# An eight-core two-layer transformer: FP4 absolute values moved to VectorE, the normalisation front split in two halves, and a constant row broadcast earlier

## The chip, the cores and the metric

The kernel runs on the 8 cores of one Trainium2 chip. Each core computes one of the 8 sequences of the batch with the same program; the cores exchange nothing. The metric is device time in microseconds (us) of the slowest core. Engines are named TensorE (PE in the profile), VectorE (DVE), ScalarE (ACT), GpSimd (POOL) and SyncE (SP, which here only issues DMAs).

## The reference

Two pre-norm layers over x of [8, 2048, 1024]. `_layernorm` here has no gain; layer 1's attention adds a second layer norm with `ln_gamma` and `ln_beta` after its own residual. The feed-forward part of layer 1 is what most of the change is about.

```python
x = x + attn0(layernorm(x))          # 16 heads, decay mask on the scores
x = x + fp6_linear(layernorm(x))     # 1024 -> 1024, blocks of 32
x = x + attn1(layernorm(x))          # its result: LN(u + attn_out) * gamma + beta
x = x + ffn1(layernorm(x))

def fp4_quant_dequant(x):            # blocks of 16 along the last dim
    scale = max(max(|xb|) / 6.0, 1e-12)
    xn = xb / scale
    idx = searchsorted([0.25, 0.75, 1.25, 1.75, 2.5, 3.5, 5.0], |xn|)
    return GRID[idx] * sign(xn) * scale
def ffn1(x):                         # H = 1024, I = 2816
    gate = fp4(x) @ fp4(w_gate).T
    y    = fp4(x) @ fp4(w_up).T
    return fp4(silu(gate) * y) @ fp4(w_down).T
```

## The kernel before

A core has 2048 rows, cut in 16 tiles of 128 rows (`NT` = 16, t = 0 to 15), one row to a partition. The program is four stages with a barrier between them: attention 0, the FP6 feed-forward layer, attention 1, the FP4 feed-forward layer (`emit_ffn1`). Intermediate results go through DRAM (`xs1` to `xs3`). The FP4 weights are quantized beforehand, in pieces woven into attention 1, by the same `emit_quant_fp4` on VectorE with 512 or 352 columns (the tiles named `pw_`).

A helper class, `Prog`, records every operation with the names of what it reads and writes, and sets semaphore waits from them. What it does not do is reorder: each engine's queue holds its operations in the order in which the Python code emits them, and an engine that waits holds back all that stands behind. The reader needs that order at every step.

`emit_ffn1` works on a tile in three parts.

- `front(t)`: load x of the tile (SyncE's queue), layer norm (`ln_stats_and_u`: a sum on VectorE at L160, a square with accumulation on ScalarE at L163, a power on GpSimd at L178, the normalised u32 by ScalarE at L182), then FP4 quantization of u32 in two halves of 512 columns into `xqb` (bf16), then eight 128x128 transposes on TensorE (L1227) through two PSUM tiles `ptr0` and `ptr1`, each copied out by ScalarE (L1230) into `xqf`.
- `back_mid(t)`: six slices k of the 2816 columns, five of 512 and one of 256. For each: eight gate matmuls (L1245), Silu on ScalarE (L1252) into `gs`, eight up matmuls (L1258), a copy on ScalarE (L1265), their product on GpSimd (L1269) back into `gs`, and FP4 quantization of `gs` on VectorE into `hq`. There are two each of the PSUM tiles `pg` and `pu`, of `gs`, and of `upe`.
- `back_down(t)`: 22 transposes of `hq` on TensorE (L1282) through the same `ptr0` and `ptr1`, each copied by ScalarE (L1285) into `hqT`; two groups of 22 matmuls of 512 columns (L1296) into `pd0` and `pd1`; an add to x on VectorE after each group (L1301); the store.

The order of the stage is written out by hand: `front(0)`, `front(1)`, `back_mid(0)`, and then for each t: `front(t+2)`, `back_mid(t+1)`, `back_down(t)`. Buffers of x and `xqf` rotate over three tiles, so x of tile t+2 goes where tile t-1 was stored from.

`emit_quant_fp4` is a chain of VectorE operations on scratch tiles that all quantizations of the stage share: block maximum (L217), scale (L220), reciprocal (L223), product y (L229), absolute value u, then four comparisons with thresholds (L240 and three times L244), three more with sums (L247 to L256), and the assembling of the result (L259 to L270). The absolute value is an activation on ScalarE (L232) when `abs_eng` is "scalar", as in all of `emit_ffn1`, and a `scalar_tensor_tensor` on VectorE (L236) by default, as in the weight preparation.

In attention 1, the row with gamma and beta is broadcast over the 128 partitions by four small fp32 matmuls with a row of ones into the one PSUM tile `pq` (L928), each copied out by ScalarE (L932) into `gb_b`. This stands after the attention proper, just before the output projection (L962), whose weights `wo` are loaded there too. `gb_b` is read by VectorE at L989 and L991. The stage begins with sixteen layer norms, whose x loads are at L700.

Of the kernel before, what the change touches and what calls it, by code (L numbers as in the profile page):

```python
# [9 lines left out]
F32 = mybir.dt.float32  # L10
BF16 = mybir.dt.bfloat16
F16 = mybir.dt.float16
AF = mybir.ActivationFunctionType
# [5 lines left out]
D = 1024  # L19
NT = T // 128  # L20
NC = D // 128
# [130 lines left out]
def ln_stats_and_u(p, xt_ap, xkey, sq_scr, sqkey, stats, stkey, col, u_out, ukey,  # L152
                   extra_u=None, rstd_via="act"):
    ncol = stats.shape[1] // 4
    s1 = stats[:, col:col + 1]
    rstd = stats[:, ncol + col:ncol + col + 1]
    negmr = stats[:, 2 * ncol + col:2 * ncol + col + 1]
    ssq = stats[:, 3 * ncol + col:3 * ncol + col + 1]
    kst = stkey + str(col) + "_"
    p.op("vector", lambda e: e.reduce_sum(s1, xt_ap, AX.X), ins=[xkey], outs=[kst + "s1"])  # L160
    p.op("vector", lambda e: e.tensor_scalar_mul(s1, s1, -1.0 / D),
         ins=[kst + "s1"], outs=[kst + "s1"])
    p.op("scalar", lambda e: e.activation(out=sq_scr, in_=xt_ap, func=AF.Square,  # L163
                                          bias=s1, accum_out=ssq),
         ins=[xkey, kst + "s1"], outs=[sqkey, kst + "ssq"])
    if rstd_via == "act":
        p.op("scalar", lambda e: e.activation(out=rstd, in_=ssq, func=AF.Ln,
                                              scale=np.float32(1.0 / D),
                                              bias=np.float32(LNEPS)),
             ins=[kst + "ssq"], outs=[kst + "rstd"])  # L170
        p.op("scalar", lambda e: e.activation(out=rstd, in_=rstd, func=AF.Exp,
                                              scale=np.float32(-0.5)),
             ins=[kst + "rstd"], outs=[kst + "rstd"])
    else:
        p.op("vector", lambda e: e.tensor_scalar(rstd, ssq, 1.0 / D, LNEPS,
                                                 ALU.mult, ALU.add),
             ins=[kst + "ssq"], outs=[kst + "rstd"])
        p.op("gpsimd", lambda e: e.tensor_tensor(rstd, rstd, p.mh[:], ALU.pow),  # L178
             ins=[kst + "rstd", "mh"], outs=[kst + "rstd"])
    p.op("vector", lambda e: e.tensor_mul(negmr, s1, rstd),  # L180
         ins=[kst + "s1", kst + "rstd"], outs=[kst + "negmr"])
    p.op("scalar", lambda e: e.activation(out=u_out, in_=xt_ap, func=AF.Identity,  # L182
                                          scale=rstd, bias=negmr),
         ins=[xkey, kst + "rstd", kst + "negmr"], outs=[ukey])
    if extra_u is not None:
        ap2, key2 = extra_u
        p.op("scalar", lambda e: e.activation(out=ap2, in_=xt_ap, func=AF.Identity,
                                              scale=rstd, bias=negmr),
             ins=[xkey, kst + "rstd", kst + "negmr"], outs=[key2])
# [395 lines left out]
def emit_attn(p, dram, layer, prep=None, prep2=None):  # L585
# [7 lines left out]
    x_d, y_d, eye_d = dram["x"], dram["y"], dram["eye"]  # L593
# [6 lines left out]
    else:  # L600
        gb_d = dram["gb"]
# [7 lines left out]
    ones32 = p.sb("ones32", [1, 128], F32)  # L609
# [49 lines left out]
    if layer == 0:  # L659
# [28 lines left out]
                                              func=AF.Identity, bias=np.float32(0.0)),  # L688
             ins=["pq"], outs=["ball"])

    outer_actx = p.actx
    with ExitStack() as sc1:
        p.actx = sc1
# [55 lines left out]
    for hp in range(NHP):  # L749
# [166 lines left out]
        in_=woT_d.ap().rearrange("(c p) f -> p c f", p=128)),  # L916
        outs=["wo"])
    if layer == 1:
        gb_b = p.sb("gb_b", [128, 2 * D], F32)
        u32 = [p.sb("u32_s", [128, D], F32)] * 2  # L920
        ysb = p.sb("ysb", [128, D], F32)
        p.dma("sync", "c_gb", lambda e: e.dma_start(out=gb_b[0:1, :],
                                                    in_=gb_d.ap()),
              outs=["gbrow"])
        for half in range(2):
            for fs in range(0, D, 512):
                o = half * D + fs
                p.op("tensor", lambda e, o=o: e.matmul(  # L928
                    pq[:, 0:512], ones32[0:1, :], gb_b[0:1, o:o + 512],
                    start=True, stop=True),  # L930
                    ins=["gbrow", "ones32"], outs=["pq"])
                p.op("scalar", lambda e, o=o: e.activation(  # L932
                    out=gb_b[:, o:o + 512], in_=pq[:, 0:512],
                    func=AF.Identity, bias=np.float32(0.0)),
                    ins=["pq"], outs=["gb_b"])
    if "dbg_attn" in dram:
        p.dma("sync", "dbg1", lambda e: e.dma_start(out=dram["dbg_attn"].ap(),
                                                    in_=attn[:]), ins=attn_all,
# [226 lines left out]
def emit_ffn1(p, dram, prep_done=False):  # L1165
# [45 lines left out]

    ISL = [(k * 512, min((k + 1) * 512, I_DIM)) for k in range(6)]

    def front(t):
        bi, ri = t % 2, t % 3
        p.dma("sync", f"x{ri}", lambda e, t=t, ri=ri: e.dma_start(
            out=xt[ri][:], in_=x_d.ap()[t * 128:(t + 1) * 128, :]),
            outs=[f"xt{ri}"])
        ln_stats_and_u(p, xt[ri][:], f"xt{ri}", u32[bi][:], "u32s",
                       stats, "st", bi, u32[bi][:], "u32s", rstd_via="pool")  # L1220
        for h in range(2):
            emit_quant_fp4(p, u32[bi][:, h * 512:(h + 1) * 512], "u32s",
                           xqb[bi][:, h * 512:(h + 1) * 512], f"xqb{bi}",
                           scr, "qs", 32, abs_eng="scalar")
        for ec in range(NC):
            pk = "ptr" + str(ec % 2)
            p.op("tensor", lambda e, ec=ec, bi=bi: e.transpose(  # L1227
                ptr[ec % 2][:], xqb[bi][:, ec * 128:(ec + 1) * 128], eye[:]),
                ins=[f"xqb{bi}", "eye"], outs=[pk])
            p.op("scalar", lambda e, ec=ec, ri=ri: e.activation(  # L1230
                out=xqf[ri][:, ec * 128:(ec + 1) * 128],
                in_=ptr[ec % 2][:], func=AF.Identity, bias=np.float32(0.0)),
                ins=[pk], outs=[f"xqf{ri}_{ec}"])

    def back_mid(t):
        bi, ri = t % 2, t % 3
        xqf_all = [f"xqf{ri}_{ec}" for ec in range(NC)]
        for k, (i0, i1) in enumerate(ISL):
            isl = slice(i0, i1)
            pgk, kpg = pg[k % 2], f"pg{k % 2}"  # L1240
            puk, kpu = pu[k % 2], f"pu{k % 2}"

            def mmg(e, isl=isl, i0=i0, i1=i1, ri=ri, pgk=pgk):
                for ec in range(NC):
                    inst = e.matmul(pgk[:, 0:i1 - i0],  # L1245
                                    xqf[ri][:, ec * 128:(ec + 1) * 128],
                                    wgT[:, ec * I_DIM:(ec + 1) * I_DIM][:, isl],
                                    start=(ec == 0), stop=(ec == NC - 1))
                return inst
            p.op("tensor", mmg, ins=xqf_all + wgT_all, outs=[kpg])  # L1250
            p.op("scalar", lambda e, i0=i0, i1=i1, k=k,
                 pgk=pgk: e.activation(  # L1252
                out=gs[k % 2][:, 0:i1 - i0], in_=pgk[:, 0:i1 - i0], func=AF.Silu),
                ins=[kpg], outs=[f"gsb{k % 2}"])

            def mmu(e, isl=isl, i0=i0, i1=i1, ri=ri, puk=puk):
                for ec in range(NC):
                    inst = e.matmul(puk[:, 0:i1 - i0],  # L1258
                                    xqf[ri][:, ec * 128:(ec + 1) * 128],
                                    wuT[:, ec * I_DIM:(ec + 1) * I_DIM][:, isl],  # L1260
                                    start=(ec == 0), stop=(ec == NC - 1))
                return inst
            p.op("tensor", mmu, ins=xqf_all + wuT_all, outs=[kpu])
            usl = slice((k % 2) * 512, (k % 2) * 512 + (i1 - i0))
            p.op("scalar", lambda e, usl=usl, i0=i0, i1=i1, puk=puk: e.activation(  # L1265
                out=upe[:, usl], in_=puk[:, 0:i1 - i0], func=AF.Identity,
                bias=np.float32(0.0)),
                ins=[kpu], outs=[f"upe{k % 2}"])
            p.op("gpsimd", lambda e, usl=usl, k=k, i0=i0, i1=i1: e.tensor_tensor(  # L1269
                gs[k % 2][:, 0:i1 - i0], upe[:, usl], gs[k % 2][:, 0:i1 - i0],  # L1270
                ALU.mult),
                ins=[f"upe{k % 2}", f"gsb{k % 2}"], outs=[f"gsb{k % 2}"])
            emit_quant_fp4(p, gs[k % 2][:, 0:i1 - i0], [f"gsb{k % 2}"],
                           hq[bi][:, isl], f"hq{bi}s_{k}", scr, "qs",
                           (i1 - i0) // 16, abs_eng="scalar")

    def back_down(t):
        bi, ri = t % 2, t % 3
# [31 lines left out]
    back_mid(0)  # L1310
    for t in range(NT):
        if t + 2 < NT:
            front(t + 2)
        if t + 1 < NT:
            back_mid(t + 1)
        back_down(t)


# [133 lines left out]
```

How the kernel before makes its waits and increments, by code:

```python
                def body(e):  # L124
                    for waits, fn, ch in recs_:
                        for typ, a, c in waits:
                            if typ == "e":
                                e.wait_ge(self.sem[a], c)
                            else:
                                e.wait_ge(self.dsem[a], 16 * c)
                        if fn is None:
                            continue
                        inst = fn(e)
                        if ch is None:
                            inst.then_inc(self.sem[eng_], 1)
                        else:
                            inst.then_inc(self.dsem[ch], 16)
```

## Time and profile before

| | |
|---|---|
| median of 3 runs | 7549.77 us (7544.5 to 7551.43) |
| the profiled execution's own time | 7555.49 us |
| its span on the slowest core (core 4), first to last instruction | 7553.9 us |
| spans of the eight cores | 7530.0 to 7553.9 us |
| VectorE, ScalarE, TensorE matmul, GpSimd busy | 62%, 29%, 38%, 2% |
| FP4 feed-forward stage, from its first weight transposes | about 5340 to 7554 us |

The profile is one execution, on the slowest core; times in it are us from the start of that core's span. About 1.6 us of the execution's time lie outside of the span. A busy share is an average over all stages. Waits are inferred from semaphores: the engine named is the one that released last.

### The profile page before, as it was taken

Reading aid. Unit: us, or ns where it says so; the run is one execution under the profiler, and the core shown is the slowest. Engines: PE = TensorE matmul, PEld = TensorE weight load, DVE = VectorE, ACT = ScalarE, POOL = GpSimd, SP = SyncE. Lnnn points to the kernel's source line nnn. Section 1 sums busy time; section 2 is a strip of 40 time slices with the busy share of each in tenths; the row PEclk is TensorE's granted clock in tenths of the full one; section 3 lists DMA queues with packets and bytes.
Section 4 is the critical chain, followed back from the end, with each engine's and each line's share of the span. In section 5 each row is a group of like instructions: output and inputs, shape, how many; then the busy total and the mean of one; then the engine's idle time right before and its main releaser. Section 6 shows DMA issues by size and latency. Waiting matters only on the chain.

```text
span 7553.9 us, 51889 instructions; the slowest of 8 cores (7530.0 to 7553.9 us)
## 1 busy us (share of the span) xinstructions
PE 2850.0 (38%) x9802; PEld 943.0 (12%) x9802; DVE 4647.5 (62%) x8046; ACT 2178.5 (29%) x3098; POOL 187.3 (2%) x193
## 2 busy tenths in 40 slices
PE   2645544445540111284343344223023333333334
PEld 1111111111110000021111111000011111111111
DVE  3555555555437777368888888843275665656555
ACT  2244544444500110244343345312111111111111
POOL 0000000000000000000000000000000000000000
PEclk9655555555575555587676677656565656656566
DMA  3000000000031110211111111111500000000000
GB/s 74 6 6 6 1 6 6 6 4 3 1 104 29 36 36 34 67 32 37 36 35 37 35 29 28 29 49 46 114 0 11 6 6 12 6 11 6 11 6 9
DMA packets 194787, 192.26 MB, mean 25 GB/s; under 512 B 120627, under 2 KB 156467, under 8 KB 194355
## 3 DMA queue, kind: packets, MB, share of 16 engines
q1 hardware_dynamic: 77332, 144.37, 5.8%
q0 software_dynamic: 39904, 25.18, 2.2%
q10 hardware_dynamic: 77248, 19.40, 1.5%
q8 instruction: 101, 1.65, 0.1%
q14 instruction: 202, 1.65, 0.1%
HBM read 133.35 MB, written 52.95 MB: 25 GB/s over the span
## 4 chain that ended last, share of the span: by engine, by line
DVE 52%; PE 15%; ACT 12%; issue 12%; DMA 6%; ACTq 2%; DVEq 2%; POOL 1%; SPq 0%; POOLq 0%
DVE f_qs_a L244 4%; DVE f_pw_a L244 4%; ACT a_ebf L829 4%; DVE a_msk L826 3%; PE a_po L843 3%; PE f_pd L1296 3%; PE a_psW L810 2%; PE a_pq L730 2%; PE a_po L848 2%; DVEq L128 2%; ACTq L564 2%; DMA f_xt<-xs 1%; DVE f_pw_y L229 1%; DVE f_pw_b L256 1%; DVE f_pw_u L236 1%
## 5 line engine op out<-in xcount | busy, mean ns | idle before, releaser
L826 DVE TENSOR_TENSOR a_msk<-a_psW,a_emask 128x1024 f32<-128x1024 f32 x512 | 623.7, 1224 | 436.8 <-PE a_psW L814 375.9
L843 PE MATMUL a_po<-a_ebf,a_v_all 128*65 128x512 bf16 x1024 | 507.4, 496 | 934.3 <-ACT a_ebf L829 777.3
L829 ACT ACTIVATE a_ebf<-a_msk 128x1024 bf16<-128x1024 f32 x512 | 541.0, 1057 | 586.5 <-DVE a_msk L826 442.3
L833 ACT ACTIVATE a_ebf<-a_psW 128x1024 bf16<-128x1024 f32 x512 | 515.0, 1023 | 110.6 <-PE a_psW L814 90.1
L848 PE MATMUL a_po<-a_ebf,a_v_all 128*65 128x512 bf16 x1024 | 516.3, 504 | 0.0
L810 PE MATMUL a_psW<-a_qp,a_kp 64*128 64x512 bf16 x1024 | 507.0, 507 | 15.6 <-ACT a_kp L776 8.4
L814 PE MATMUL a_psW<-a_qp,a_kp 64*128 64x512 bf16 x1024 | 507.5, 508 | 0.0
L232 ACT ACTIVATE f_qs_u<-f_qs_y 128x512 f32<-128x512 f32 (+1 forms) x128 | 77.1, 602 | 1134.3 <-DVE f_qs_y L229 1134.3
L244 DVE SCALAR_TENSOR_TENSOR f_qs_a<-f_qs_u,f_qs_a 128x512 f32<-128x512 f32 (+1 forms) x384 | 313.9, 817 | 40.3 <-DVE f_qs_a L244 0.5
L894 PE MATMUL a_pq<-a_dbf,a_ones 1*64 1x512 bf16 x64 | 38.4, 600 | 764.3 <-ACT a_dbf L885 764.3
L1245 PE MATMUL f_pg<-f_wgT,f_xqf 128*128 128x512 bf16 (+1 forms) x768 | 233.8, 465 | 235.2 <-ACT f_gs L1252 235.2
L244 DVE SCALAR_TENSOR_TENSOR f_pw_a<-f_pw_u,f_pw_a 128x512 f32<-128x512 f32 (+1 forms) x456 | 283.6, 622 | 49.9 <-DVE f_pw_a L244 1.8
L1227 PE MATMUL f_ptr<-f_eye,f_xqb 128*128 128x128 bf16 x128 | 30.5, 264 | 739.6 <-DVE f_xqb L270 719.2
L1087 PE MATMUL f_ptr<-f_eye,f_xqb 128*128 128x128 bf16 x128 | 32.5, 264 | 713.1 <-DVE f_xqb L346 693.6
L1282 PE MATMUL f_ptr<-f_eye,f_hq 128*128 128x128 bf16 x352 | 88.6, 266 | 535.8 <-ACT f_hqT L1285 527.3
L843 PEld LDWEIGHTS a_po<-a_ebf,a_v_all 128*65 128x65 bf16 x1024 | 122.3, 119 | 1349.1 <-issue 1349.1
L962 PE MATMUL a_psW<-a_wo,a_attn 128*128 128x512 bf16 x512 | 164.5, 479 | 279.3 <-DVE a_ysb L984 218.9
L769 PE MATMUL a_pq<-a_u_fm,a_wqkv 128*128 128x512 bf16 x1024 | 256.5, 418 | 0.0
L866 ACT ACTIVATE a_asb<-a_po 64x512 f32<-64x512 f32 x64 | 37.8, 591 | 630.5 <-DVE a_attn L878 629.6
L1258 PE MATMUL f_pu<-f_wuT,f_xqf 128*128 128x512 bf16 (+1 forms) x768 | 203.5, 418 | 0.0
L1296 PE MATMUL f_pd<-f_wdT,f_hqT 128*128 128x512 bf16 x704 | 194.5, 447 | 8.5 <-ACT f_hqT L1285 8.5
L1090 ACT ACTIVATE f_xqf<-f_ptr 128x128 bf16<-128x128 bf16 x128 | 33.7, 277 | 552.7 <-PE f_ptr L1087 551.5
(196 smaller groups left out, 6072.1 us busy)
## 6 DMA issues: line engine op xcount, KB each, us to landing
xs<-a_xtw SPq DMA_DIRECT2D x32, 512.0 KB, 2.6
f_xt<-xs SPq DMA_DIRECT2D x32, 512.0 KB, 3.8
f_pw_wch<-f_wg SPq DMA_DIRECT2D x44, 256.0 KB, 2.8
f_pw_wch<-f_wu SPq DMA_DIRECT2D x44, 256.0 KB, 2.8
f_pw_wch<-f_wd SPq DMA_DIRECT2D x64, 176.0 KB, 2.4
a_xt<-x SPq DMA_DIRECT2D x16, 512.0 KB, 3.8
a_xtw<-x SPq DMA_DIRECT2D x16, 512.0 KB, 3.5
f_xtw<-xs POOLq DMA_DIRECT2D x16, 512.0 KB, 3.6
```

What stands on the lines that cost most here:

```text
L244: p.op("vector", lambda e, th=th: e.scalar_tensor_tensor(out=a[:, 0:W], in0=u[:, 0:W], scalar=th, in1=a[:, 0:W], op0=ALU.is_gt, op1=ALU.ad ...
L769: inst = e.matmul(psel[:], wqkv[wb][:, j * D + c * 128: j * D + c * 128 + 128], u_fm[:, c * T:(c + 1) * T][:, sl], start=(c == 0), stop=(c ...
L810: p.op("tensor", lambda e, kc=kc, psx=psx, qsl=qsl: e.matmul(psx[:, 0:512], kp[0:64, kc * 128:(kc + 1) * 128], qp[0:64, qsl], start=True, ...
L814: p.op("tensor", lambda e, kc=kc, psx=psx, qsl=qsl: e.matmul(psx[:, 512:1024], kp[64:128, kc * 128:(kc + 1) * 128], qp[64:128, qsl], start ...
L826: p.op("vector", lambda e, m3=m3, p3=p3, e3=e3: e.tensor_tensor(m3, p3, e3, ALU.mult), ins=[kA, kB, "emask0", "emask1"], outs=[f"mskp{par}"])
L829: p.op("scalar", lambda e, esl=esl: e.activation(out=ebf[:, esl], in_=msk[:, esl], func=AF.Exp), ins=[f"mskp{par}"], outs=[ek])
L833: p.op("scalar", lambda e, psx=psx, esl=esl: e.activation(out=ebf[:, esl], in_=psx[:], func=AF.Exp, scale=np.float32(0.125)), ins=[kA, kB] ...
L843: p.op("tensor", lambda e, kc=kc, eo=eo, vb=vb: e.matmul(po0[0:65, :], v_all[:, vb: vb + 65], ebf[:, eo: eo + 512], start=(kc == 0), stop= ...
L848: p.op("tensor", lambda e, kc=kc, eo=eo, vb=vb: e.matmul(po1[0:65, :], v_all[:, vb + 65: vb + 130], ebf[:, eo + 512: eo + 1024], start=(kc ...
L1245: inst = e.matmul(pgk[:, 0:i1 - i0], xqf[ri][:, ec * 128:(ec + 1) * 128], wgT[:, ec * I_DIM:(ec + 1) * I_DIM][:, isl], start=(ec == 0), st ...
L1258: inst = e.matmul(puk[:, 0:i1 - i0], xqf[ri][:, ec * 128:(ec + 1) * 128], wuT[:, ec * I_DIM:(ec + 1) * I_DIM][:, isl], start=(ec == 0), st ...
L1296: inst = e.matmul(psx[:], hqT[:, ic * 128:(ic + 1) * 128], wdT[:, ic * D:(ic + 1) * D][:, fsl], start=(ic == 0), stop=(ic == NI - 1))
```

## The change

It does four things.

- In `emit_ffn1` all quantizations take the absolute value on VectorE (L236) in place of ScalarE (L232): `abs_eng="scalar"` goes away in both calls.
- `front(t)` becomes `front_half(t, 0)` and `front_half(t, 1)`. Half 0 has the load, the layer norm, the quantization of columns 0 to 511 and the first four transposes with their copies; half 1 has the quantization of columns 512 to 1023 and the other four.
- In the loop, half 0 of tile t+2 stays ahead of `back_mid(t+1)`, and half 1 comes after it, ahead of `back_down(t)`. The two fronts at the start of the stage have both halves in a row.
- In attention 1 the load, the four matmuls and the four copies of gamma and beta go to the beginning of the stage, ahead of the sixteen layer norms; `gb_b` is held from there on.

```diff
--- before.py
+++ after.py
@@ -688,6 +688,23 @@
                                               func=AF.Identity, bias=np.float32(0.0)),
              ins=["pq"], outs=["ball"])
 
+    if layer == 1:
+        gb_b = p.sb("gb_b", [128, 2 * D], F32)
+        p.dma("sync", "c_gb", lambda e: e.dma_start(out=gb_b[0:1, :],
+                                                    in_=gb_d.ap()),
+              outs=["gbrow"])
+        for half in range(2):
+            for fs in range(0, D, 512):
+                o = half * D + fs
+                p.op("tensor", lambda e, o=o: e.matmul(
+                    pq[:, 0:512], ones32[0:1, :], gb_b[0:1, o:o + 512],
+                    start=True, stop=True),
+                    ins=["gbrow", "ones32"], outs=["pq"])
+                p.op("scalar", lambda e, o=o: e.activation(
+                    out=gb_b[:, o:o + 512], in_=pq[:, 0:512],
+                    func=AF.Identity, bias=np.float32(0.0)),
+                    ins=["pq"], outs=["gb_b"])
+
     outer_actx = p.actx
     with ExitStack() as sc1:
         p.actx = sc1
@@ -916,23 +933,8 @@
         in_=woT_d.ap().rearrange("(c p) f -> p c f", p=128)),
         outs=["wo"])
     if layer == 1:
-        gb_b = p.sb("gb_b", [128, 2 * D], F32)
         u32 = [p.sb("u32_s", [128, D], F32)] * 2
         ysb = p.sb("ysb", [128, D], F32)
-        p.dma("sync", "c_gb", lambda e: e.dma_start(out=gb_b[0:1, :],
-                                                    in_=gb_d.ap()),
-              outs=["gbrow"])
-        for half in range(2):
-            for fs in range(0, D, 512):
-                o = half * D + fs
-                p.op("tensor", lambda e, o=o: e.matmul(
-                    pq[:, 0:512], ones32[0:1, :], gb_b[0:1, o:o + 512],
-                    start=True, stop=True),
-                    ins=["gbrow", "ones32"], outs=["pq"])
-                p.op("scalar", lambda e, o=o: e.activation(
-                    out=gb_b[:, o:o + 512], in_=pq[:, 0:512],
-                    func=AF.Identity, bias=np.float32(0.0)),
-                    ins=["pq"], outs=["gb_b"])
     if "dbg_attn" in dram:
         p.dma("sync", "dbg1", lambda e: e.dma_start(out=dram["dbg_attn"].ap(),
                                                     in_=attn[:]), ins=attn_all,
@@ -1211,18 +1213,18 @@
 
     ISL = [(k * 512, min((k + 1) * 512, I_DIM)) for k in range(6)]
 
-    def front(t):
+    def front_half(t, h):
         bi, ri = t % 2, t % 3
-        p.dma("sync", f"x{ri}", lambda e, t=t, ri=ri: e.dma_start(
-            out=xt[ri][:], in_=x_d.ap()[t * 128:(t + 1) * 128, :]),
-            outs=[f"xt{ri}"])
-        ln_stats_and_u(p, xt[ri][:], f"xt{ri}", u32[bi][:], "u32s",
-                       stats, "st", bi, u32[bi][:], "u32s", rstd_via="pool")
-        for h in range(2):
-            emit_quant_fp4(p, u32[bi][:, h * 512:(h + 1) * 512], "u32s",
-                           xqb[bi][:, h * 512:(h + 1) * 512], f"xqb{bi}",
-                           scr, "qs", 32, abs_eng="scalar")
-        for ec in range(NC):
+        if h == 0:
+            p.dma("sync", f"x{ri}", lambda e, t=t, ri=ri: e.dma_start(
+                out=xt[ri][:], in_=x_d.ap()[t * 128:(t + 1) * 128, :]),
+                outs=[f"xt{ri}"])
+            ln_stats_and_u(p, xt[ri][:], f"xt{ri}", u32[bi][:], "u32s",
+                           stats, "st", bi, u32[bi][:], "u32s", rstd_via="pool")
+        emit_quant_fp4(p, u32[bi][:, h * 512:(h + 1) * 512], "u32s",
+                       xqb[bi][:, h * 512:(h + 1) * 512], f"xqb{bi}",
+                       scr, "qs", 32)
+        for ec in range(h * 4, h * 4 + 4):
             pk = "ptr" + str(ec % 2)
             p.op("tensor", lambda e, ec=ec, bi=bi: e.transpose(
                 ptr[ec % 2][:], xqb[bi][:, ec * 128:(ec + 1) * 128], eye[:]),
@@ -1231,6 +1233,10 @@
                 out=xqf[ri][:, ec * 128:(ec + 1) * 128],
                 in_=ptr[ec % 2][:], func=AF.Identity, bias=np.float32(0.0)),
                 ins=[pk], outs=[f"xqf{ri}_{ec}"])
+
+    def front(t):
+        front_half(t, 0)
+        front_half(t, 1)
 
     def back_mid(t):
         bi, ri = t % 2, t % 3
@@ -1272,7 +1278,7 @@
                 ins=[f"upe{k % 2}", f"gsb{k % 2}"], outs=[f"gsb{k % 2}"])
             emit_quant_fp4(p, gs[k % 2][:, 0:i1 - i0], [f"gsb{k % 2}"],
                            hq[bi][:, isl], f"hq{bi}s_{k}", scr, "qs",
-                           (i1 - i0) // 16, abs_eng="scalar")
+                           (i1 - i0) // 16)
 
     def back_down(t):
         bi, ri = t % 2, t % 3
@@ -1310,9 +1316,11 @@
     back_mid(0)
     for t in range(NT):
         if t + 2 < NT:
-            front(t + 2)
+            front_half(t + 2, 0)
         if t + 1 < NT:
             back_mid(t + 1)
+        if t + 2 < NT:
+            front_half(t + 2, 1)
         back_down(t)
```

## Rows read from the trace of the kernel before

**Rows 1.** The page, parts 1 and 4: busy time by engine, the chain that ended last.

```profile
PE 2850.0 (38%) x9802; PEld 943.0 (12%) x9802; DVE 4647.5 (62%) x8046; ACT 2178.5 (29%) x3098; POOL 187.3 (2%) x193
...
DVE 52%; PE 15%; ACT 12%; issue 12%; DMA 6%; ACTq 2%; DVEq 2%; POOL 1%; SPq 0%; POOLq 0%
```

**Rows 2.** Waits in the last stage: who waited for whom, total us, times, longest.

```profile
DVE f_xt L1301 <- PE f_pd L1296: 249.3, 31, 16.0
...
DVE f_qs_bm L217 <- POOL f_gs L1269: 177.0, 16, 11.7
```

**Rows 3.** Timeline of one tile, VectorE: start, us, engine, line, operation, [idle before <-releaser].

```profile
5609.29 0.69 DVE L270 TENSOR_TENSOR f_xqb<-f_qs_a,f_qs_b 128x512 bf16<-128x512 f32 x1
...
5620.64 0.69 DVE L217 TENSOR_REDUCE f_qs_bm<-f_gs 128x32 f32<-128x512 f32 x1 [10.66 <-POOL f_gs L1269]
...
5689.73 0.42 DVE L270 TENSOR_TENSOR f_hq<-f_qs_a,f_qs_b 128x256 bf16<-128x256 f32 x1
...
5701.18 0.69 DVE L1301 TENSOR_TENSOR f_xt<-f_pd,f_xt 128x512 f32<-128x512 f32 x1 [11.02 <-PE f_pd L1296]
...
5705.99 0.69 DVE L1301 TENSOR_TENSOR f_xt<-f_pd,f_xt 128x512 f32<-128x512 f32 x1 [4.12 <-PE f_pd L1296]
...
5752.99 0.69 DVE L217 TENSOR_REDUCE f_qs_bm<-f_gs 128x32 f32<-128x512 f32 x1 [11.42 <-POOL f_gs L1269]
```

**Rows 4.** Timeline of the same tile, TensorE.

```profile
5610.12 0.37 PE L1227 MATMUL f_ptr<-f_eye,f_xqb 128*128 128x128 bf16 x2 [66.91 <-DVE f_xqb L270]
...
5613.08 3.62 PE L1245 MATMUL f_pg<-f_wgT,f_xqf 128*128 128x512 bf16 x8
...
5684.80 0.50 PE L1282 MATMUL f_ptr<-f_eye,f_hq 128*128 128x128 bf16 x2 [31.82 <-ACT f_hqT L1285]
...
5693.92 11.90 PE L1296 MATMUL f_pd<-f_wdT,f_hqT 128*128 128x512 bf16 x44 [0.52 <-ACT f_hqT L1285]
```

**Rows 5.** Timeline: one quantization of the last stage, and one of the weight preparation.

```profile
4908.68 0.53 DVE L236 SCALAR_TENSOR_TENSOR f_pw_u<-f_pw_y 128x352 f32<-128x352 f32 x1
4909.31 0.34 DVE L240 TENSOR_SCALAR f_pw_a<-f_pw_u 128x352 f32<-128x352 f32 x1
...
5634.61 0.69 DVE L229 TENSOR_TENSOR f_qs_y<-f_gs,f_qs_bm 128x512 f32<-128x512 f32 x1
...
5636.13 0.43 DVE L240 TENSOR_SCALAR f_qs_a<-f_qs_u 128x512 f32<-128x512 f32 x1 [0.83 <-ACT f_qs_u L232]
...
5636.66 3.15 DVE L244 SCALAR_TENSOR_TENSOR f_qs_a<-f_qs_u,f_qs_a 128x512 f32<-128x512 f32 x3
...
5637.14 1.33 POOL L1269 TENSOR_TENSOR f_gs<-f_upe,f_gs 128x512 f32<-128x512 f32 x1 [11.10 <-ACT f_upe L1265]
```

**Rows 6.** Timeline of the last two tiles.

```profile
7482.43 0.59 ACT L1265 ACTIVATE f_upe<-f_pu 128x512 f32<-128x512 f32 x1
...
7510.87 0.42 DVE L270 TENSOR_TENSOR f_hq<-f_qs_a,f_qs_b 128x256 bf16<-128x256 f32 x1
...
7538.17 11.38 PE L1296 MATMUL f_pd<-f_wdT,f_hqT 128*128 128x512 bf16 x44 [0.62 <-ACT f_hqT L1285]
...
7549.73 0.69 DVE L1301 TENSOR_TENSOR f_xt<-f_pd,f_xt 128x512 f32<-128x512 f32 x1 [4.13 <-PE f_pd L1296]
```

**Rows 7.** Timeline of layer 1's attention: its start, and gamma and beta's place.

```profile
3060.35 0.91 SPq L700 DMA_DIRECT2D a_xt<-xs  x2
...
3065.52 1.15 ACT L163 ACTIVATE a_msk<-a_xt,a_stats 128x1024 f32<-128x1024 f32 x1 [24.63 <-DVE a_stats L161]
...
4975.09 0.26 SPq L922 DMA_DIRECT2D a_gb_b<-a_gb  x1
...
4978.29 2.04 PE L928 MATMUL a_pq<-a_gb_b,a_ones 1*128 1x512 f32 x2 [117.07 <-DMA a_gb_b<-a_gb]
...
4989.39 0.60 ACT L932 ACTIVATE a_gb_b<-a_pq 128x512 f32<-128x512 f32 x1 [2.38 <-PE a_pq L928]
...
4991.69 3.57 PE L962 MATMUL a_psW<-a_wo,a_attn 128*128 128x512 bf16 x8 [2.40 <-DMA a_wo<-a_woT]
```

## The prediction

> **What bounds the kernel now.** I read the page first, for the shares. VectorE is busy 62% of the span and holds 52% of the chain that ended last [rows 1]; no other engine comes near. Most of the diff is in the last stage (the FP4 feed-forward layer), so I then read the waits of VectorE in that stage [rows 2]. Two recur once per tile: the residual adds (L1301) wait for the down projection, 249.3 us over 31 waits, and the first quantization of a tile (L217) waits for the gate and up results through GpSimd, 177.0 us over 16. Then I followed one tile in the timeline [rows 3]. It begins at 5620.64 and the next begins at 5752.99, so a tile takes 132.35 us: six quantizations of `back_mid` (to 5690.15), 11.02 us of wait, one add, 4.12 us of wait, one add (to 5706.68), a layer norm and two quantizations of `front`, and 11.42 us of wait. VectorE is either working or waiting for a chain that its own last result started. So the stage is serial, and the question for each edit is what it does to these waits.
>
> Why they exist is in the queues of TensorE and ScalarE [rows 4]. TensorE stood idle for 66.91 us until `front(t+2)`'s last quantization wrote `xqb`, and then ran its transposes and after them `back_mid(t+1)`'s gate matmuls at 5613.08. Those need only activations of tile t+1, ready one tile before; they waited because they stand behind the transposes. TensorE takes its queue strictly in the order of the program. At 5684.80 the transposes of `hq` (tile t) resume after 31.82 us, released by ScalarE: the copies out of PSUM (L1285) stand behind the last absolute value (L232) of tile t+1, which waits for VectorE. The down projection starts at 5693.92, and its first half frees the add at 5701.18.
>
> **Absolute value on VectorE (128 quantizations of the last stage).** Now L240 starts 1.52 us after L229 (5634.61 to 5636.13), of which 0.83 us is idle for ScalarE's result [rows 5]. After, L236 stands between them. No row has it with 512 columns. The weight preparation has it with 352: 0.53 us, and L240 follows 0.63 us after it, a gap of 0.10. L229 itself takes 0.69 for 512, on two operands as L236 has. So 0.69 + 0.10, twice, is 1.58 us: +0.06 for each of seven full quantizations of a tile, and about +0.02 for the one of 256 columns, in all +0.44 us per tile. Bounds: 0 (the idle time is just filled), and 0.2 for each (a gap twice as long on both sides), 1.5 per tile.
>
> Perfetto Trace Analysis of the Trainium skill, section Optimizing Scalar/DVE Operations, speaks against this edit: when VectorE is saturated, offloading some work to ScalarE may make sense. The trace doesn't bear it out here, since VectorE waits 0.83 us for what was offloaded.
>
> GpSimd's multiply (L1269) is moved too. It runs beside L244 [rows 5]: the three L244 take 3.15 us where 3 x 0.69 + 2 x 0.10 = 2.27 would do, so it costs VectorE 0.88 us, four times per tile (0.3 for the fifth, short one). Without the absolute value in ScalarE's queue, the Silu and the copy that feed it run about 0.54 us earlier, and the multiply starts at some 5636.6 instead of 5637.14, just ahead of the first L244 instead of late in it. VectorE then stands blocked from closer to the multiply's beginning: I estimate +0.18 each, +0.7 per tile. Bounds: -0.88 (no overlap) and +0.45 (blocked for the whole 1.33), so -3.5 to +1.8 per tile.
>
> The SBUF — State Buffer page of the Trainium skill, under Who interferes with whom, says that VectorE and GpSimd share a port pair as an exclusive lock. By that rule a multiply costs VectorE at most its own 1.33 us; the sum would be the upper bound just given.
>
> The larger effect is on order: ScalarE's copies of `hq` no longer stand behind the last absolute value. By itself this would let them run during `back_mid(t+1)`.
>
> **Split front (14 tiles have it).** After quantizing half 0, only four transposes are queued before `back_mid(t+1)`'s gate matmuls. Eight took 5613.08 - 5610.12 = 2.96 us from first to gate; in steady pace a pair starts every 0.89 us, so four fewer are 1.8 us: the wait of 11.42 shrinks to 9.6. Bound: 0.9, if the clock (0.43 us per matmul, the 1.2 GHz level, in the gate group that took 3.62 us) rises no earlier than it does now. I take -1.8.
>
> But half 1's quantization now comes after all six of `back_mid(t+1)`, and its four transposes stand in TensorE's queue ahead of `back_down(t)`'s 22. So `hq(t)` is held until VectorE has ended half 1; VectorE's next instruction is the add that needs the down projection. Nothing covers it. From the end of half 1: 0.15 us to the first transpose (as before 5610.12); 26 transposes in 13 pairs. Twenty took 5693.92 - 5684.80 = 9.12 us to the down projection; six more at 0.445 each give 11.8. Then 5701.18 - 5693.92 = 7.26 to the add. That is 19.2 us of wait in place of 11.02: +8.2 us. The second wait, 4.12, stays. What was gained on ScalarE is unused, because the copies wait for transposes that TensorE has not run. The next tile's x load stays behind the store, as now.
>
> Per tile: +8.2 - 1.8 + 0.44 + 0.7 = +7.5 us, and 14 tiles give +105. The start (two fronts, one `back_mid`) gives -1.8 + 0.6 + 0.7 = -0.5.
>
> **The end.** Tiles 14 and 15 have no front above them, so there ScalarE's freedom counts [rows 6]. The last quantization of tile 15 ends at 7511.29. ScalarE reached the copy of slice 4 at 7482.43; with the absolute values gone slice 5's is done about then. 22 transposes (10 us) and 12.8 us of down projection of tile 14 are over by about 7506, and 20 of tile 15's transposes by 7515. Its down projection starts near 7515.3 instead of 7538.17: -22.9, and +1.2 for the quantizations before it: -21.7.
>
> **Gamma and beta.** Four rounds of matmul and copy took 4978.29 to 4989.99, 11.7 us, beginning 3.2 us after the row's DMA was issued at 4975.09 [rows 7]. At their old place they are free: the output projection starts at 4991.69 when its weights land. At the new one ScalarE's first square (3065.52) stands behind them. The row is issued where now the first x load is, at 3060.35, so they end near 3075.1: +9.6. VectorE's next step needs that square, so nothing hides it. I add 0.6 for a first output projection without the warm-up that those matmuls gave: +10.2. Bounds: 8 to 11.5.
>
> **Sum.** 105 - 0.5 - 21.7 + 10.2 = +93 us. The profiled execution took 7555.49, 5.7 over the median; +93 on it is 7648.5, and on the median 7549.8 it is 7643.
>
> **Rivals.**
> - *The down projection hides under the second half* (ends faster). If the `hq(t)` transposes ran while VectorE quantizes tile t+1, the 11.02 and 4.12 would vanish: -15.1 - 1.8 + 0.44 + 0.7 = -15.8 per tile, -221 for 14; with the other terms -233, that is 7317. This decides at one point: whether they get ahead of the four second-half transposes. For it: their data are ready a tile early, and ScalarE is free. Against it: the 66.91 us of idle TensorE with ready work queued behind [rows 4]. 6 in 100.
> - *The low clock lasts through the down projection.* All 44 matmuls at 0.43 would take 18.9 us instead of 12.8, from 5693.92 to 5706.68: +6.1, for 14 tiles +86, 7729. The transposes before it are sparse now too, and the rise came inside it, so I give 5 in 100.
> - *VectorE pays the absolute value in full*, as the rule on offloading has it: 112 x 0.69 + 16 x 0.42 = 84 us instead of 7, giving 7720. The 0.83 of idle time speaks against it. 3 in 100.
> - *It about cancels.* The multiplies stop colliding (64 x 0.88 + 16 x 0.3 = -61 us, and -11 that I had added), which leaves +21, 7571. If TensorE's clock rises early in the down projection as well (2.7 us of low clock saved is 1.3 per tile, -18), it is +3, 7553. 6 in 100, two thirds of it within 0.2%.
> - The forecast has 80 in 100.
>
> **How the numbers follow.** Against the values taken, the multiplies' bounds are -59 and +15 us over 14 tiles, those of the absolute value -6 and +15, that of the split's saving +13, and a clock that rises 2.7 us earlier or later in the down projection is 18 either way. All at once is unlikely; half of each is -42 and +31, and I widen the upper side to +42, since late clocks and late multiplies would come together. That gives 7600 to 7685, which should hold 8 in 10 over all cases: the forecast nearly whole, and little of the rivals. 0.2% is 15 us, about what a measurement of this kernel can tell from no change. Faster 0.06, same 0.04, slower 0.90.
>
> **What would show it.** The adds' first wait should read about 19 us per tile instead of 11, released by a down projection that starts some 12 us after half 1's last write. L217's wait should be near 9.6. TensorE should stand idle through `back_mid(t+1)` until L1227's second half, and L1282 should never run before it except in tile 14. L240 should wait for nothing. The layer's first square should start near 3075. The forecast is wrong if L1282 runs beside `back_mid`, if the three L244 change their 3.15 us by more than half, or if the down projection takes over 15 us.

## The result, and the profile after

The changed kernel takes 7624.55 us (median of 8 runs, 7612.9 to 7652.61) against 7550.78 us before (8 runs, 7544.5 to 7565.5): a ratio of 1.01, 95% interval 1.0085 to 1.0114. It is slower by 74 us; the forecast was slower by 93, 7643 in a range of 7600 to 7685.

The page's busy times and chain hardly tell the two kernels apart [rows 1]. VectorE is busy 94 us more, ScalarE 67 less:

```profile
PE 2789.1 (37%) x9802; PEld 929.5 (12%) x9802; DVE 4741.6 (62%) x8174; ACT 2111.3 (28%) x2970; POOL 180.8 (2%) x193
...
DVE 53%; PE 16%; issue 11%; ACT 11%; DMA 5%; ACTq 2%; DVEq 2%; POOL 1%; SPq 0%; POOLq 0%
```

The waits of VectorE in the last stage do (total us, times, longest). They answer to [rows 2]: the adds' wait for the down projection grew from 249.3 to 341.0, the first quantization's fell from 177.0 to 146.1.

```profile
DVE f_xt L1307 <- PE f_pd L1302: 341.0, 30, 19.5
...
DVE f_qs_bm L217 <- POOL f_gs L1275: 146.1, 16, 9.8
```

One tile on VectorE, as in [rows 3]. The first row is now half 1's last write, the next two are the adds, and the last begins the next tile:

```profile
5674.40 0.69 DVE L270 TENSOR_TENSOR f_xqb<-f_qs_a,f_qs_b 128x512 bf16<-128x512 f32 x1
...
5694.38 0.69 DVE L1307 TENSOR_TENSOR f_xt<-f_pd,f_xt 128x512 f32<-128x512 f32 x1 [19.29 <-PE f_pd L1302]
...
5699.20 0.69 DVE L1307 TENSOR_TENSOR f_xt<-f_pd,f_xt 128x512 f32<-128x512 f32 x1 [4.12 <-PE f_pd L1302]
...
5732.73 0.69 DVE L217 TENSOR_REDUCE f_qs_bm<-f_gs 128x32 f32<-128x512 f32 x1 [9.39 <-POOL f_gs L1275]
```

And TensorE, as in [rows 4]:

```profile
5675.24 0.37 PE L1229 MATMUL f_ptr<-f_eye,f_xqb 128*128 128x128 bf16 x2 [62.80 <-DVE f_xqb L270]
...
5677.01 0.52 PE L1288 MATMUL f_ptr<-f_eye,f_hq 128*128 128x128 bf16 x2 [0.40 <-ACT f_xqf L1232]
...
5687.19 11.83 PE L1302 MATMUL f_pd<-f_wdT,f_hqT 128*128 128x512 bf16 x44 [0.52 <-ACT f_hqT L1291]
```

TensorE waits 62.80 us for half 1, runs four transposes, begins the 22 of `hq` at 5677.01 and the down projection at 5687.19. The add waits 19.29 us, behind nothing but these. Where [rows 4] had ScalarE as the releaser of the `hq` transposes after 31.82 us, TensorE's own queue now holds them.

From the traces' times I worked out stretches of the stages, as means over the eight cores, in us. Each runs from one DMA issue or first instruction to the next.

```
stretch                                                 before    after
attention 1: load of bq to load of the v weights          141.6    150.6
attention 1: to the load of the output weights           1775.5   1766.1
attention 1: to the last stage's first weight transpose   364.4    363.4
last stage: to the first square of a layer norm            99.0     99.3
last stage: to the first quantization of back_mid          69.4     65.6
last stage: from there to the end                        2042.9   2118.3
```

Two things stand out. The last row has the loss, 75 us. And attention 1 lost 9 us at its beginning and found them again in its middle, where the change touches nothing.

### The profile page after: what moved, and what is told of

The parts are those of the page before. It is cut to its first block, busy times and chain, and to the rows that moved or that the text cites. A ratio compares the mean times of both kernels' runs of the same rounds, so it can differ in the third digit from the quotient of the medians.

```text
span 7614.2 us, 51936 instructions; the slowest of 8 cores (7602.4 to 7614.2 us)
## 1 busy us (share of the span) xinstructions
PE 2789.1 (37%) x9802; PEld 929.5 (12%) x9802; DVE 4741.6 (62%) x8174; ACT 2111.3 (28%) x2970; POOL 180.8 (2%) x193
## 4 chain that ended last, share of the span: by engine, by line
DVE 53%; PE 16%; issue 11%; ACT 11%; DMA 5%; ACTq 2%; DVEq 2%; POOL 1%; SPq 0%; POOLq 0%
DVE f_qs_a L244 4%; ACT a_ebf L846 4%; DVE f_pw_a L244 4%; PE a_po L860 3%; DVE a_msk L843 3%; PE a_psW L827 2%; PE f_pd L1302 2%; PE a_po L865 2%; DVEq L128 2%; PE a_pq L747 2%; ACTq L564 1%; DVE f_qs_u L236 1%; DMA f_xt<-xs 1%; DVE f_pw_y L229 1%; DVE f_pw_u L236 1%
## 5 line engine op out<-in xcount | busy, mean ns | idle before, releaser
L850 ACT ACTIVATE a_ebf<-a_psW 128x1024 bf16<-128x1024 f32 x512 | 511.2, 1023 | 114.3 <-PE a_psW L831 94.8
L244 DVE SCALAR_TENSOR_TENSOR f_qs_a<-f_qs_u,f_qs_a 128x512 f32<-128x512 f32 (+1 forms) x384 | 299.2, 779 | 41.4 <-DVE f_qs_a L244 1.8
L244 DVE SCALAR_TENSOR_TENSOR f_pw_a<-f_pw_u,f_pw_a 128x512 f32<-128x512 f32 (+1 forms) x456 | 283.6, 622 | 47.5
L1307 DVE TENSOR_TENSOR f_xt<-f_pd,f_xt 128x512 f32<-128x512 f32 x32 | 22.1, 692 | 341.1 <-PE f_pd L1302 341.0
L1251 PE MATMUL f_pg<-f_wgT,f_xqf 128*128 128x512 bf16 (+1 forms) x768 | 204.8, 420 | 80.4 <-ACT f_gs L1258 80.4
L1258 ACT ACTIVATE f_gs<-f_pg 128x512 f32<-128x512 f32 x96 | 53.9, 562 | 632.0 <-DVE f_qs_y L229 537.0
```

The source lines that it names most:

```text
L244: p.op("vector", lambda e, th=th: e.scalar_tensor_tensor(out=a[:, 0:W], in0=u[:, 0:W], scalar=th, in1=a[:, 0:W], op0=ALU.is_gt, op1=ALU.ad ...
L850: p.op("scalar", lambda e, psx=psx, esl=esl: e.activation(out=ebf[:, esl], in_=psx[:], func=AF.Exp, scale=np.float32(0.125)), ins=[kA, kB] ...
L1251: inst = e.matmul(pgk[:, 0:i1 - i0], xqf[ri][:, ec * 128:(ec + 1) * 128], wgT[:, ec * I_DIM:(ec + 1) * I_DIM][:, isl], start=(ec == 0), st ...
```

## Experiments

Ratios are to the kernel before, run on the same chip.

**1. Gamma and beta early, nothing else.** The diff's first hunk and the removal of its lines at the old place.

> The kernel before with gamma and beta's broadcast moved to the beginning of attention 1, nothing else. By the sum of the prediction the first square of the stage starts some 9 us later and nothing hides it: about +9 us, near 7560, and the span from the stage's first load to the output projection's weights is 9 us longer. The rival comes from the changed kernel's profile, where attention 1 as a whole was not longer (2280.1 us against 2281.5, means over cores) though its beginning was by 9: by that the 9 us are given back later in the stage, 7550, and the eight head pairs should then each be about 1.2 us shorter here too. If the head pairs take what they took before, the difference in the changed kernel was one of executions.

Measured: 7547.86 us, ratio 1.0001 (0.9993 to 1.001). My sum's +9 did not come, and its rival held. The beginning of attention 1 is 8.9 us longer (150.5), its middle 9.2 us shorter (1766.3): the changed kernel's finding again, and spread over all eight head pairs, 0.3 to 1.6 us each. So it belongs to the edit, and is no accident of an execution. What it is, runs 5 and 6 ask.

**2. Absolute values on VectorE alone.**

```diff
-                           scr, "qs", 32, abs_eng="scalar")
+                           scr, "qs", 32)
...
-                           (i1 - i0) // 16, abs_eng="scalar")
+                           (i1 - i0) // 16)
```

> The kernel before with all absolute values of the last stage on VectorE, fronts whole, gamma and beta where they were. My theory: ScalarE's copies of hq now run beside back_mid, so the adds' waits (15.1 us per tile) vanish, against +0.9 us per tile in back_mid: about -14.4 us for 14 tiles and -22 at the end, near 7327. The rival that VectorE pays the absolute value in full (77 us) and the copies gain nothing gives 7627.

Measured: 7313.12 us, ratio 0.969 (0.9677 to 0.9703). Its waits on VectorE in the last stage:

```profile
DVE f_qs_bm L217 <- POOL f_gs L1269: 165.2, 15, 12.0
...
DVE f_xt L1301 <- PE f_pd L1296: 13.0, 2, 8.9
```

The adds wait twice, at the end of the program, and never else. A tile takes 118.1 us instead of 133.0. Against the kernel before on the same chip (7548.45 us) this edit was worth 235 us, and in the change it earned only the end of the program.

**3. The split alone**, absolute values on ScalarE.

> The kernel before with the front split as in the change, absolute values on ScalarE, gamma and beta where they were. My theory (half 1's four transposes hold back the 22 of back_down in TensorE's queue): from the end of back_mid to the second add +8.0 us beyond the moved quantization, first wait of a tile -2.0, so +6.0 for 14 tiles, about +82, near 7632, with nothing gained at the end (39 us from the last quantization to the last add, as before). If the absolute value were what costs, this would be at or below 7530.

Measured: 7627.6 us, ratio 1.0106 (1.009 to 1.0121).

```profile
DVE f_xt L1305 <- PE f_pd L1300: 361.6, 31, 20.3
DVE f_qs_bm L217 <- POOL f_gs L1273: 145.5, 16, 9.9
```

361.6 and 145.5 us, the pattern of the changed kernel. From the last quantization to the last add it takes 39.0 us, as before the change.

**4. The changed kernel, half 1's four transposes behind `back_down`.**

```diff
         if t + 2 < NT:
             front_half(t + 2, 1)      # its quantization only
         back_down(t)
+        if t + 2 < NT:
+            front_tr(t + 2, 1)        # its four transposes and copies
```

> The changed kernel with one thing moved: half 1 is quantized where the change has it, but its four transposes stand behind back_down's work in TensorE's and ScalarE's queues. My theory says that these four are the whole cause: the adds' wait of 19.3 + 4.1 us goes to nothing and a tile takes about 116.5 us instead of 140.0, near 7296 in all. If instead TensorE's clock or VectorE's extra work were behind the slower tile, it would stay near 7620.

Measured: 7291.57 us, ratio 0.9659 (0.9646 to 0.9673).

```profile
DVE f_qs_bm L217 <- POOL f_gs L1281: 142.8, 16, 9.9
...
DVE f_xt L1313 <- PE f_pd L1308: 12.4, 2, 8.3
```

A tile takes 116.1 us. VectorE does the same work in the same order as in the changed kernel; only four transposes per tile, with their copies, have another place in TensorE's and ScalarE's queues, and the time falls by 333 us.

**5 and 6. One more VectorE instruction.** In the traces, the 9 us found again are small idle times of VectorE inside the weight preparation. Where two operations of a quantization usually stand 0.10 us apart, at some places it is 0.46, as in this row of the kernel before (VectorE's timeline at the second such place, [idle before]):

```profile
3403.51 0.35 DVE L223 RECIPROCAL f_pw_bm<-f_pw_bm 128x32 f32<-128x32 f32 x1 [0.46 <-DVE f_pw_bm L220]
```

The place is not bound to an operation. Numbering all entries of VectorE's instruction list from 0 (waits too), every such stall of every kernel sits at an entry number that is 59 modulo 128, and this entry is an operation with its wait just ahead of it. The weight preparation has 41 entries with such a number. In the kernel before 35 of them are operations, of which 29 stall; in the changed one 8 are, and 4 stall. The others have no wait just ahead, but for three L217. The edit for both runs:

```diff
+    if layer == 1:
+        fill = p.sb("fill", [1, 1], F32)
+        p.op("vector", lambda e: e.memset(fill[:], 0.0), outs=["fill"])
```

> The kernel before with one more instruction for VectorE, a memset of one element at the beginning of attention 1, which needs about 0.1 us. In the traces so far VectorE stands idle for 0.46 us in the weight preparation 29 times in each kernel with gamma and beta in their old place, 4 times in each with them at the new one, on every core alike, and each time at an entry of its instruction list whose number is 59 modulo 128; the two kinds of kernels differ there by one entry. Theory: where the entry that follows such a place is the operation itself and not its wait, 0.46 us is exposed, and one more entry takes 25 of the 29 stalls away: about -9 us, near 7540, with 4 stalls. The rival (the place of gb_b in memory, or the clock) expects no change, 7549, with 29.

> The changed kernel with the same one-element memset. Theory: the 4 stalls of its weight preparation become some 29 again or another number between, at most +9 us, near 7633. The rival expects 7624 and 4 stalls.

Measured, kernel before with the memset: 7539.14 us, ratio 0.9987 (0.9978 to 0.9996), 4 stalls on every core, and the middle of attention 1 takes 1766.5 us instead of 1775.5. Changed kernel with it: 7630.43 us, ratio 1.011 (1.0096 to 1.0124), 29 stalls, and the middle takes 1773.7 instead of 1766.1. Its time alone could not be told from the changed kernel's; the stretch and the stalls can. Of the waits of VectorE on its own last result, the kernel before with the memset keeps four rows between 3200 and 4975 us (its waits of 0.5 us are the 4 stalls; the three of L223, of 0.3 each, stand just behind an entry numbered 59 that is a wait, where part of the stall still shows), where the changed one with it has eleven, which make up the 29, and of which the first four are:

```profile
DVE f_pw_b L250 <- DVE f_pw_b L247: 0.9, 2, 0.5
DVE f_pw_bm L223 <- DVE f_pw_bm L220: 0.8, 3, 0.3
DVE f_pw_b L263 <- DVE f_pw_b L259: 0.5, 1, 0.5
DVE f_pw_a L268 <- DVE f_pw_u L265: 0.5, 1, 0.5
```

```profile
DVE f_pw_a L244 <- DVE f_pw_a L244: 2.3, 5, 0.5
DVE f_pw_wqb L270 <- DVE f_pw_a L268: 1.8, 4, 0.5
DVE f_pw_u L236 <- DVE f_pw_y L229: 1.4, 3, 0.5
DVE f_pw_bm L223 <- DVE f_pw_bm L220: 1.4, 3, 0.5
...
```

So the place of VectorE's entries is the cause of the 9 us: the same memset takes the stalls from one kernel and gives them to the other. What moved the list by one entry in the change is the broadcast's DMA: its channel is waited for at the barrier after the layer norms, one wait more ahead of the preparation and one fewer after it (16301 entries in the kernel before and in run 1).

**7. Transposes late, fronts whole**, on the kernel before with the absolute values on VectorE:

```diff
         if t + 2 < NT:
-            front(t + 2)
+            front_dve(t + 2)          # load, layer norm, both quantizations
         if t + 1 < NT:
             back_mid(t + 1)
+        if t + 2 < NT:
+            front_tr(t + 2)           # eight transposes and copies
         back_down(t)
```

> The kernel before with absolute values on VectorE, and fronts whole but for their eight transposes, which stand between back_mid(t+1) and back_down(t). My theory of in-order queues: the gate matmuls of tile t+1 no longer stand behind transposes that wait for VectorE, so the wait of about 11.4 us ahead of the first quantization vanishes besides the adds' waits: a tile takes 106.9 us where it took 118.2 with the absolute values alone, near 7155 in all. The rival is that the 30 transposes with their copies and the down projection no longer fit beside back_mid(t+1); then the adds wait again for some us per tile, 7155 to 7250.

Measured: 7171.07 us, ratio 0.95 (0.9487 to 0.9513). The adds and the first quantization wait twice each, outside of the steady tiles. A tile takes 107.8 us where I expected 106.9. Of this 0.9 us, 0.5 is that the wait that vanished was 10.9 us in run 2, and I had taken 11.4. Two products per tile now run beside VectorE's work of the front, where in run 2 only one stood there and met its wait. But they cost little in all: L236, L240 and L244 are stretched by 4.4 us per tile, against 4.3 in run 2. What remains is open. The first row below, the wait for the load of x, is what run 8 takes up.

```profile
DVE f_stats L160 <- DMA f_xt<-xs: 88.6, 14, 9.1
...
DVE f_xt L1312 <- PE f_pd L1307: 12.1, 2, 8.0
DVE f_qs_bm L217 <- POOL f_gs L1280: 11.8, 2, 10.9
```

**8. Early loads** on top of it, with the memset. A fourth buffer for x lets each load be issued a tile earlier; the first three loads stand ahead of `front(0)`:

```diff
-    xt = [... for i in range(3)]
+    xt = [... for i in range(4)]
...
     for t in range(NT):
+        if t + 3 < NT:
+            load_x(t + 3)
```

> The kernel of the run with late transposes, with four x buffers in the last stage and each x loaded one tile ahead, and with the one-element memset in attention 1. The wait of 6.1 us for x vanishes from 13 tiles (-79 us), and the memset gives what it gives to the kernel before (about -9): near 7067, a tile in 100.8 us. If the load is not what the layer norm waits for, it stays near 7146.

Measured: 7077.03 us, ratio 0.9378 (0.9365 to 0.9391), 10 us over the 7067 expected; a tile takes 101.5 us where I expected 100.8.

**9 and 10. The product on VectorE**, in the changed kernel and in that of run 8: `"gpsimd"` to `"vector"` at L1275 of the changed kernel.

> The changed kernel with the product of Silu and up results (GpSimd's multiply) done by VectorE. It measures what the meeting of the two engines costs. By my reading the multiplies stretch VectorE's L236, L240 and L244 by 4.3 us per tile (their means are 818, 505 and 830 ns where undisturbed ones take 692, 427 and 692), and five products of 0.79 and one of 0.53 cost VectorE 4.5; the first quantization of a tile starts 0.6 earlier. So about -0.4 us per tile, near 7618, and L244 at 692 ns throughout. If the stretching had another cause, the products would come on top: +62 us, near 7687, with L244 still at 830.

> The same edit on the kernel with late transposes and early loads. By my reading the two sides cancel here too (-4.6 and +4.5 per tile, and no wait ahead of the first quantization to shorten): within 10 us of 7077. If the stretching had another cause: +72, near 7149.

Measured: 7602.68 us, ratio 1.0071 (1.0056 to 1.0086), and 7071.82 us, ratio 0.9369 (0.9353 to 0.9385). Groups of VectorE's instructions in 5592.3 to 7412 us (busy, mean ns), first of the changed kernel, then of run 9:

```profile
L244 DVE SCALAR_TENSOR_TENSOR f_qs_a<-f_qs_u,f_qs_a 128x512 f32<-128x512 f32 x273 | 226.5, 830 | 29.4 <-DVE f_qs_a L244 1.4
L236 DVE SCALAR_TENSOR_TENSOR f_qs_u<-f_qs_y 128x512 f32<-128x512 f32 x91 | 74.4, 818 | 9.4
L240 DVE TENSOR_SCALAR f_qs_a<-f_qs_u 128x512 f32<-128x512 f32 x91 | 45.9, 505 | 10.0 <-DVE f_qs_u L236 0.5
```

```profile
L244 DVE SCALAR_TENSOR_TENSOR f_qs_a<-f_qs_u,f_qs_a 128x512 f32<-128x512 f32 x276 | 191.0, 692 | 29.8 <-DVE f_qs_a L240 0.9 <-DVE f_qs_a L244 0.5
L236 DVE SCALAR_TENSOR_TENSOR f_qs_u<-f_qs_y 128x512 f32<-128x512 f32 x92 | 63.7, 692 | 9.6
L240 DVE TENSOR_SCALAR f_qs_a<-f_qs_u 128x512 f32<-128x512 f32 x92 | 39.3, 427 | 9.8
```

Without GpSimd's multiply all three have their undisturbed lengths, so the stretching was the meeting of the two engines and nothing else. Run 9 gained 22 us where I expected 6 (tiles of 138.8 instead of 139.9). The two kernels ran on different chips and their intervals touch, but the last stretch of the last stage is 20 us shorter too (2098.5 for 2118.3). Part of it are tiles of about 137.4 us among others of 139.4, in which the first add waits some 18.4 us instead of 19.7; run 3 has such tiles too, and I did not settle what makes them. Run 10 has the lowest median of the study, at 0.9369 of the kernel before, but its interval overlaps that of run 8, so the product's place made no difference there that could be told.

## Why the prediction was right, point by point

**The mechanism held.** Half 1's transposes hold back the down projection. From the end of `back_mid` to the second add it took 16.9 us before and 36.5 after, medians over the tiles; less the moved quantization of 11.6 that is +8.0, where the step said +8.2, and the wait row reads 19.29 where it said 19.2. Run 3 has the same loss with the absolute values untouched, and run 4 takes it away, with what ScalarE's freedom brings, by moving these four transposes alone. The forecast did not name what that freedom is worth by itself, though its first rival priced it: 7317, and run 4 measured 7291.57.

**Front.** From the second add to the next tile's first quantization, 46.45 us before, 32.85 and the moved 11.6 after: -2.0, forecast -1.8.

**Absolute value and multiplies.** `back_mid` takes 70.6 us instead of 69.7: +0.9, forecast 0.3 and 0.7. The row for one quantization, which answers to [rows 5]:

```profile
5608.03 0.69 DVE L236 SCALAR_TENSOR_TENSOR f_qs_u<-f_qs_y 128x512 f32<-128x512 f32 x1
...
5608.82 0.43 DVE L240 TENSOR_SCALAR f_qs_a<-f_qs_u 128x512 f32<-128x512 f32 x1
...
5609.24 1.27 POOL L1275 TENSOR_TENSOR f_gs<-f_upe,f_gs 128x512 f32<-128x512 f32 x1 [9.79 <-ACT f_upe L1271]
5609.36 3.29 DVE L244 SCALAR_TENSOR_TENSOR f_qs_a<-f_qs_u,f_qs_a 128x512 f32<-128x512 f32 x3
```

L236 to L240 takes 0.79, as worked out from the 352 columns. The multiply starts 0.12 us ahead of the first L244, as forecast, and the three take 3.29 us, +0.14 on 3.15. But this row stands for three of the five multiplies of a tile that meet VectorE. The other two now start earlier than I had thought and meet L236 and L240 (shown at the end), so the mean L244 fell to 830 ns. It was 877 before, from 5620.6 to 7441.7 us:

```profile
L244 DVE SCALAR_TENSOR_TENSOR f_qs_a<-f_qs_u,f_qs_a 128x512 f32<-128x512 f32 x288 | 252.6, 877 | 30.3 <-DVE f_qs_a L244 0.5
```

Over L236, L240 and L244 together the stretching is 4.3 us per tile instead of 3.8: +0.5 where the sum had +0.7. The size was nearly right, the picture behind it right only in part.

The Trainium skill (Perfetto Trace Analysis, Optimizing Scalar/DVE Operations) says that offloading some work to ScalarE may make sense when VectorE is saturated, which speaks against this edit. Run 2 shows it worth 235 us here, since what limited VectorE were waits. The Trainium skill's page SBUF — State Buffer (Who interferes with whom) has the port lock hold VectorE for no longer than GpSimd's operation runs, and the trace agrees: 0.69 to 1.57 us is 0.88 more (below), and the multiply takes 1.27.

A tile is +6.9 (139.9 for 133.0 in the mean) where the sum said +7.5: 14 tiles 97 us, not 105.

**The end.** From the first quantization of tile 15's `back_mid` to the last add, 108.6 us became 86.8: -21.8, forecast -21.7.

**The beginning of the last stage** gave -3.8 us where the sum had -1.8 (its -0.5 also counts the quantizations of `back_mid(0)`). TensorE's part came as forecast: the wait ahead of the first quantization of `back_mid(0)` fell from 11.0 to 9.0. But the layer norm of tile 1 used to stand behind all eight copies of tile 0 in ScalarE's queue, and now stands behind four: from tile 0's last write to tile 1's first L217 it is 5.9 us instead of 7.6. I had counted only TensorE's part.

**The term that was mis-sized: gamma and beta.** I put +10.2 us. The layer norm's first square does come late as forecast; here it is 13.4 us after the first x load's issue at 3049.36, and was 5.2 [rows 7]:

```profile
3062.80 1.14 ACT L163 ACTIVATE a_msk<-a_xt,a_stats 128x1024 f32<-128x1024 f32 x1
...
4981.63 3.57 PE L964 MATMUL a_psW<-a_wo,a_attn 128*128 128x512 bf16 x8 [129.76 <-DMA a_wo<-a_woT]
```

That part measured +9.0. But the other end of the same stage gave 9.4 back, which no row of the kernel before announced to me, and runs 1, 5 and 6 put on the place of VectorE's instructions in their list. My 0.6 for a lost warm-up is a term that no run shows: the first eight matmuls of the output projection take 3.57 us with the broadcast's matmuls ahead of them [rows 7] and without, and the stretch after them is 1.0 shorter. Attention 1 as a whole: -1.4 us.

Together the steps give 97 - 3.8 - 21.8 - 1.4 = 70 us, against 74 measured and 93 forecast. The errors all lie on one side and none hid another: 8 us in the tiles, 3 at the beginning of the stage, 12 in attention 1.

## What to carry to other kernels

An instruction that waits holds back everything behind it in its engine's queue, so write next to each emitted block which engine's result its first instruction waits for, and put what waits longest last. Freeing an engine (here ScalarE) brings nothing while the queue that feeds it is still held: absolute values moved alone gave 235 us, and the same edit with four transposes ahead of the down projection lost 74. A wait that repeats with every tile is best answered by the order of emission before any operation is made cheaper.

## What the runs showed of the hardware that was not expected

VectorE loses 0.36 us at some places that come every 128 entries of its instruction list, where the entry numbered 59 modulo 128 is an operation with its wait just ahead of it. It is the same on all eight cores, and one added memset took 25 of 29 away and 9.0 us from the stage. Why entries come in 128s, the runs do not show. The Trainium skill (Runtime: NRT & Kernel Launch, Instruction fetch mechanics) has instructions fetched in blocks of 256 at a mostly hidden cost; if these stalls are that, which no run here shows, the block and the cost differ. For a comparison of kernels within 0.2% it matters: an edit anywhere ahead moves all later stalls.

The multiply on GpSimd lengthens a VectorE operation that starts while it runs, and not only L244. In the changed kernel's timeline of all engines, L240 (0.43 alone) and L236 (0.69 alone):

```profile
5634.47 0.72 POOL L1275 TENSOR_TENSOR f_gs<-f_upe,f_gs 128x256 f32<-128x256 f32 x1 [11.31 <-ACT f_upe L1271]
5634.48 1.00 DVE L240 TENSOR_SCALAR f_qs_a<-f_qs_u 128x512 f32<-128x512 f32 x1
...
5734.82 1.27 POOL L1275 TENSOR_TENSOR f_gs<-f_upe,f_gs 128x512 f32<-128x512 f32 x1 [2.19 <-ACT f_upe L1271]
5735.06 1.57 DVE L236 SCALAR_TENSOR_TENSOR f_qs_u<-f_qs_y 128x512 f32<-128x512 f32 x1
```

L240 starts 0.01 us after the multiply and takes 1.00; L236 starts 0.24 after it and takes 1.57. In run 9 there is no such row.
